# A graph-transformer layer on one core: inputs normalised twice and turned directly, VectorE's first-stage work in another order, four staging rows for keys, mixer weights asked for sooner

## What is computed

```python
xn = _layernorm(x)
x = x + gnn(xn, edges) + mix(xn)          # the two branches read the same xn
x = x + ffn(_layernorm(x))
# gnn(x):
x_norm = _layernorm(x, ln_g, ln_b)        # a second normalisation, on xn
q, k, v = (x_norm @ W + b).reshape(N, 8, 64) for each of Wq, Wk, Wv
ws = (q[src] . k[dst]) * SCALE * edge_attr_8
att = softmax of ws over the edges of one src
values = segment_sum(att * v[dst], src)
return x + (values @ W1 + b1) @ W2 + b2
# mix(x): linear attention with Wq, Wk, Wv, Wp of its own, over all rows
```

## Time and profile before

| | us |
|---|---|
| median of 3 runs (880.22 to 887.66) | 885.28 |
| the profiled execution | 888.54 |
| its span in the trace | 886.8 |
| PE busy | 805.7 (91%) |
| DVE busy | 583.9 (66%) |
| POOL busy | 460.3 (52%) |
| ACT busy | 343.4 (39%) |

### The profile page before, as it was taken

How to read it: one execution, slowest core, us unless ns; L and a number is a source line. 1 busy time by engine, 2 the same in 40 slices (tenths; PEclk the granted TensorE clock), 3 DMA queues, 4 the chain that set the end, 5 groups by cost and what they waited for, 6 DMA issues and landing times.

```text
span 886.8 us, 13753 instructions
## 1 busy us (share of the span) xinstructions
PE 805.7 (91%) x4791; PEld 464.8 (52%) x4791; DVE 583.9 (66%) x1331; ACT 343.4 (39%) x794; POOL 460.3 (52%) x391
## 2 busy tenths in 40 slices
PE   2999997868999999799999999999999999999974
PEld 2554446434456444355555555555556666666642
DVE  3587493924232502277877787888998888788775
ACT  0412301022312131055545555455556555454462
POOL 1038887887878878778778787876100000000000
PEclk9989999988999999889999999999999999999987
DMA  7698999996445476033533535335442323323103
GB/s 220 191 372 273 314 312 306 289 346 205 112 112 159 124 235 215 5 99 99 194 100 111 182 100 193 99 109 181 157 154 100 113 101 105 140 83 105 63 1 116
DMA packets 69635, 144.02 MB, mean 162 GB/s; under 512 B 20537, under 2 KB 54251, under 8 KB 65599
## 3 DMA queue, kind: packets, MB, share of 16 engines
q1 hardware_dynamic: 47084, 119.42, 38.0%
q0 software_dynamic: 13344, 6.28, 6.3%
q10 hardware_dynamic: 9136, 17.39, 5.9%
HBM read 77.99 MB, written 64.77 MB: 161 GB/s over the span
## 4 chain that ended last, share of the span: by engine, by line
PE 66%; DVE 16%; issue 8%; ACT 5%; DMA 4%; ACTq 1%; DVEq 0%
PE bank L890 15%; PE bank L884 10%; DVE AR L1538 9%; PE bank L1099 8%; PE bank L1117 7%; PE bank L1085 7%; PE bank L1145 4%; PE bank L1090 4%; ACT AR L765 3%; DMA AR<-in_L_mix_Wk_dram 2%; PE bank L998 2%; PE bank L873 1%; DMA AR<-in_L_gnn_b_dram 1%; PE bank L987 1%; PE bank L949 1%
## 5 line engine op out<-in xcount | busy, mean ns | idle before, releaser
L514 POOL DMA_INDIRECT w_tab<-pay,idx x330 | 406.3, 1231 | 153.0 <-issue 152.4
L765 ACT ACTIVATE AR<-AR,nmx 128x512 f32<-128x512 f32 (+1 forms) x240 | 159.5, 665 | 179.8 <-DVE nmx L1542 144.4
L1538 DVE CUSTOM_DVE_ANT_0 AR<-bank,AR,MX 128x512 f32<-128x512 f32 (+1 forms) x160 | 151.4, 985 | 23.5 <-PE bank L1090 21.3
L1099 PE MATMUL bank<-ident,AR 128*128 128x128 f32 (+2 forms) x880 | 133.8, 282 | 13.9 <-ACT AR L765 10.5
L1085 PE MATMUL bank<-KT,QT 64*128 64x512 f32 (+1 forms) x480 | 118.8, 572 | 14.3 <-issue 8.6
L1099 PEld LDWEIGHTS bank<-ident,AR 128*128 128x128 f32 (+2 forms) x880 | 98.2, 140 | 61.6 <-ACT AR L765 47.2
L884 PE MATMUL bank<-AR 128*128 128x512 f32 (+1 forms) x288 | 108.6, 537 | 7.8 <-ACT QT L642 3.5
L1117 PE MATMUL bank<-AR,V 128*64 128x128 f32 (+1 forms) x1600 | 114.4, 281 | 0.4 <-DVE AR L1549 0.4
L890 PE MATMUL bank<-AR 128*128 128x512 f32 x240 | 110.4, 616 | 2.5 <-ACT AR L696 2.5
L1538 DVE CUSTOM_DVE_ANT_0 AR<-bank,AR 128x512 f32<-128x512 f32 x80 | 83.9, 1088 | 38.5 <-PE bank L1090 25.8
L587 POOL DMA_INDIRECT AR<-kv_rows,xd x10 | 10.7, 1070 | 188.2 <-PE bank L1117 179.2
(11 more groups left out here) (250 smaller groups left out, 759.2 us busy)
## 6 DMA issues: line engine op xcount, KB each, us to landing
w_tab<-ztile SPq DMA_DIRECT2D x20, 2280.0 KB
AR<-w_tab SPq DMA_DIRECT2D x20, 2048.0 KB
AR<-w_tab SPq DMA_DIRECT2D x10, 1344.0 KB
w_tab<-ztile SPq DMA_DIRECT2D x3, 1800.0 KB
w_tab<-pay,idx POOLq DMA_INDIRECT x330
w_tab<-ztile SPq DMA_DIRECT2D x2, 1700.0 KB
kv_rows<-AR ACTq DMA_DIRECT2D x9, 256.0 KB
kv_rows<-V ACTq DMA_DIRECT2D x9, 256.0 KB
```

Of the source, the lines that this page charges most:

```text
L514: pool.indirect_dma_start(out=w_tab, out_offset=bass.IndirectOffsetOnAxis(ap=idx[:, k, j:j + 1], axis=0), in_=pay[:, k % RING, j, :], in_o ...
L765: act.activation(ws[u % 2][hh][:, 0:n], ws[u % 2][hh][:, 0:n], ACT.Exp, bias=nmx[:, u % 4, hh:hh + 1], accum_out=DG[g][:, c, 2 * p + hh:2 ...
L1099: last = nc.tensor.transpose(bank[2 + hh][0:rws, i * P:(i + 1) * P], ws[u % 2][hh][:, a:a + rws], ident[:, :])
L1538: v.tensor_tensor_reduce(out=ws[u % 2][hh][:, 0:n], in0=bank[SB[(2 * u + hh) % 3]][:, 0:n], in1=Wt[w % 2][:, 0:n, h], scale=1.0, scalar=MX ...
```

## The change

- `normed_twice(j)` writes the rows normalised with both row scales at once (`r12 = r1 * r2`) to the staging tile; PE turns them, and the column scale and shift are applied as they are taken from PSUM (`take_x2`, on ACT, and for piece 0 half on DVE). `spread`, `gain_row` and `fold` go. The rows normalised once are written and turned later, by a second set of transposes per piece.
- DVE's list of the first stage is written in another order: `detect`, the checks, `take_k`, `take_v` and `moments` stand elsewhere; `take_k` and `take_v` of piece 2 are spread over the loser lists.
- Four staging rows for keys instead of two.
- The loads of the mixer's Wk and Wv are issued ahead of the last `k_rows`, `residual(j)` behind `k_rows`. `loser_bases` and `loser_columns` stand earlier on PE.
- The check's copy of the edge weights, `wchk`, lies in tiles 4 to 9 of `V` instead of 0 to 5. `dwin` lies where it was.

The diff, cut to its core:

```diff
-        stg = [ar(19520 + 512 * i, 512) for i in range(2)]
+        stg = [ar(19520, 512), ar(20032, 512), QMN[:, 1760:2272], QMN[:, 2272:2784]]
...
-        wchk = V[0:QL, 0:6, :].rearrange("p t d -> p (t d)")[:, 0:330 * H].rearrange("p (t h) -> p t h", h=H)
+        wchk = V[0:QL, 4:NT, :].rearrange("p t d -> p (t d)")[:, 0:330 * H].rearrange("p (t h) -> p t h", h=H)
...
+            def take_x2(j, ks):
                 t0, n = PIECES[j]
+                if j == 2:
+                    act.wait_ge(s_pr, PROJ_OF["v", 3] + 1)
+                act.wait_ge(s_cols, 1)
+                for k in ks:
+                    tau = TAU_OF["x2", j, k]
+                    act.wait_ge(s_tt, tau + 1)
+                    act.activation(x2T[j % 2][:, k, 0:n * P], bank[tau % 2][:, 0:n * P], ACT.Identity,
+                                   bias=cols[:, 1, k:k + 1], scale=cols[:, 0, k:k + 1]).then_inc(s_ta[tau % 2], 1)
...
             for j in range(3):
                 take_q(j)
                 if j < 2:
-                    gain_row(j + 1)
-                    take_x(j + 1)
+                    take_x2(j + 1, range(KC))
                 if j == 0:
                     roots(2)
-                if j < 2:
-                    residual(j + 1)
+                elif j == 2:
+                    act.dma_start(sMk, wv(mWk)).then_inc(s_mk_l, 16)
+                    act.wait_ge(s_pr, PROJ_OF["k", 2, KC - 1] + 1)
+                    act.dma_start(sMv, wv(mWv)).then_inc(s_mv_l, 16)
+                take_x(j)
                 t0, n = PIECES[j]
                 for t in range(t0, t0 + n):
                     k_rows(t)
+                residual(j)
...
+            def normed_twice(j):
+                t0, n = PIECES[j]
+                a, b = t0, t0 + n
+                if j:
+                    dve.wait_ge(s_tt, TAU_OF[("x2", 0, KC - 1) if j == 1 else ("x", 0, KC - 1)] + 1)
+                dve.wait_ge(s_sq2, j + 1)
+                ch.link(v.reciprocal(r2[:, a:b], sq[:, 1, a:b]))
+                ch.link(v.tensor_tensor(r12[:, a:b], r1[:, a:b], r2[:, a:b], ALU.mult))
+                for i in range(n):
+                    t = t0 + i
+                    v.tensor_scalar(ta[:, i, :], XRES[:, t, :], MV[:, t, 0:1], r12[:, t:t + 1], ALU.subtract, ALU.mult).then_inc(s_xn2, 1)
...
-            normed(0)
             dve.wait_ge(s_cols, 1)
-            take_x(0)
-            fold(0)
+            v.tensor_scalar(qbias[:, :], cols[:, 2, :], SCALE, None, ALU.mult).then_inc(s_qb, 1)
+            normed_twice(0)
+            take_x2(0, (0, 2))
             moments(1)
-            normed(1)
+            normed_twice(1)
             edges()
-            detect(0)
-            detect(1)
-            fold(1)
-            order_checks()
             for m in range(KC):
                 take_k(0, m)
-                detect(2 + m)
+                detect(m)
             moments(2)
-            take_x(1)
-            fold(2)
-            marker_check()
+            normed(0)
+            dve.wait_ge(s_row, 48)
             for t in range(4):
                 take_v(t)
-                if t == 1:
-                    normed(2)
-                detect(6 + t)
+                detect(4 + t)
+            normed_twice(2)
+            order_checks()
+            detect(8)
+            detect(9)
+            normed(1)
+            marker_check()
```

More of the change, by code:

```diff
@@ L87, in link @@
         self.eng.wait_ge(self.sem, self.n)
[L90 removed]
+TAU = [("x2", 0, k) for k in range(KC)]
 for _j, (_t0, _n) in enumerate(PIECES):
     if _j < 2:
[L93 removed]
+        TAU += [("x2", _j + 1, k) for k in range(KC)]
+    TAU += [("x", _j, k) for k in range(KC)]
     TAU += [("k", _t0 + i) for i in range(_n)]
@@ L576, in _ @@
             pool.wait_ge(s_xd, 1)
-            for i in range(2):
-                pool.wait_ge(s_kvst[i], 16 * NT // 2)
+            for i in range(4):
+                pool.wait_ge(s_kvst[i], 16 * ((NT + 3 - i) // 4))
             pool.wait_ge(s_vst, 16 * NT)
@@ L829, in _, with transpose_x @@
             mm = nc.tensor.matmul
-            def spread(j):
+            def transpose_x(what, j):
                 t0, n = PIECES[j]
-                pe.wait_ge(s_r2, j + 1)
-                if j:
-                    pe.wait_ge(s_r2b, j)
-                for i in range(n):
-                    last = nc.tensor.transpose(bank[6][:, i * P:(i + 1) * P], r2[:, t0 + i:t0 + i + 1].to_broadcast([P, P]), ident[:, :])
-                last.then_inc(s_r2p, 1)
-            def take(tau):
-                if tau >= 2:
-                    pe.wait_ge(s_ta, tau - 1)
-            def transpose_x(j):
-                t0, n = PIECES[j]
-                pe.wait_ge(s_xn, t0 + n)
+                pe.wait_ge(s_xn2 if what == "x2" else s_xn, t0 + n)
                 for k in range(KC):
-                    tau = TAU_OF["x", j, k]
-                    take(tau)
+                    tau = TAU_OF[what, j, k]
+                    if tau >= 2:
+                        turned(pe, tau - 2)
                     for i in range(n):
@@ L881, in qk @@
                 for m in range(KC):
+                    if what == "mq" and j == 0 and m == 2:
+                        loser_columns()
                     b = proj((what, j, m))
@@ L1315, in _ @@
                 detect(10 + t)
-            for m in range(KC):
-                take_k(2, m)
-                detect(18 + m)
-            for t in range(8, NT):
-                take_v(t)
-            place_checks()
             def whole(out_, in_, less, per):
@@ L1329, in _ @@
             flat = lambda a: a.rearrange("p k j -> p (k j)")
+            normed(2)
+            for k in range(18, NCH):
+                detect(k)
+            place_checks()
+            take_k(2, 0)
             for i, c in enumerate((dc, oc)):
+                take_k(2, 1 + i)
                 ch.link(v.tensor_tensor(e1, flat(c[:, :, :]), steps1250[0:QL, :], ALU.add))
@@ L1354, in _ @@
             v.tensor_reduce(tot, oc1, AX.X, ALU.add).then_inc(s_tot, 1)
+            take_v(9)
             dve.wait_ge(s_tot, 1)
@@ L1400, in _ @@
             dve.wait_ge(s_pr, PROJ_OF["v", NT - 1] + 1)
-            for i in range(2):
-                dve.wait_ge(s_kvst[i], 16 * NT // 2)
+            for i in range(4):
+                dve.wait_ge(s_kvst[i], 16 * ((NT + 3 - i) // 4))
             for i in range(2):
```

149 lines of the change are left out of this document (52 added, 97 removed).

## The result

| | before | changed |
|---|---|---|
| median, us | 886.47 (880.22 to 888.11, 4 runs) | 11495.80 (11490.46 to 11499.04, 4 runs) |
| span of the profiled execution, us | 886.8 | 11497.3 |
| time over time of before | | 12.99, 95% interval 12.95 to 13.03 |

The change makes the kernel 13 times slower. The flag is set, and every engine runs the general path. That was the forecast: 9850 us, with 7700 to 12,800 around it. The place and the chain were as predicted; a pass takes 31.05 us and not 26, at the upper edge of the 22 to 31 us that the forecast gave it.

The account below looks back on a forecast made before the run. PE, busy 91%, bounds the kernel; the change sets the flag and brings the general path: 616.7 + 50 + 8580 (330 passes of 26 us) + 85 + 515 + 1.7 = 9850 us, range 7700 to 12,800.

Parts of the forecast that it names:

- what the change does to the flag: DVE's first stage: take_k overwrites the destinations' copy in KT before its comparison, 13 of 22 windows; flag is 125.
- The frame of the sum: Time around the loop: entry at 616.7 us, 50 ahead of it, 85 behind, attention 515, 1.7 around the span.
- three gathers: POOL's one-element operation and three gathers at a pass's start: 7.7 us, lower 5.5, upper 12.9.
- scatter: POOL's state scatter of 264 KB at a pass's end: 4.3 us with its one-element operation, lower 3.0.
- handovers: Ten handovers between engines and the loop's registers in a pass: 1.0 us, an estimate.
- The rule of the Trainium skill: 450 KB gather: 2.0 us plus bytes over 436 GB/s, 3.0 us; a pass 3 us shorter, 8850 us in all.
- Rival 3: Long pass: code fetched again at each jump back adds 5 to 9 us, 31 to 35 a pass, 11500 to 12800; 20%.
- its own case: General path's loop: 330 passes of 26 us, 22 to 31 us a pass, 9850 us in all; 60%.
- The quiet flag: Checks still come out 0 and the general path is not run: 867 us; 3%.
- The wait of 3.5 us for ACT goes with four staging rows: PE ahead of the attention stage: its 3.5 us wait goes, part of about 30 us won without the flag.
- the 6.8 us that the loser columns were to save: PE ahead of the attention stage: waits of 6.8 and 2.5 us go with earlier weights and loser columns.
- The cap: Attention stage, tile 10: POOL's pace lets at most 23 us of the lead be kept without the flag.

Follow-up runs that it names:

- e1: The changed kernel with order_checks() directly behind edges(), ahead of the first take_k; 872.54 us, 0.985 of before.
- e2: The kernel before with one move alone, order_checks() behind the four take_k of piece 0; 11467.47 us.
- e3: e1 with column 1 of viol overwritten by ones behind the second check; 11479.62 us.
- e12: The changed kernel in its own order, with the copy of the destinations where no key of piece 0 is written; 0.971 of before.
- e6: The changed kernel with 112 rows instead of 125 in each of a pass's four DMAs; 9585.55 us.
- e7: e1 with detect(0) directly behind edges() and ACT's load of the mixer's Wq issued later, behind roots(2); 869.45 us, 0.981 of before.
- e4: The changed kernel whose passes leave out the gather of the state rows; 11239.62 us.

## Why the prediction was right, and its wrong steps

**The flag** came out as predicted, by the step "what the change does to the flag": e1, e2, e3 and e12 show that the cells shared by `dwin` and the first keys set it, and nothing else. Which of the two comparisons set it, and that it stands at 125, was worked out and not read from any run: the branch asks only whether the flag is over 0.

**The frame of the sum.** Entry at 621.2 us instead of 616.7: POOL's last scatter came 2.9 us later, and from its end to the first DMA of `general()` went 2.9 where I had 1.3 (the rows that I read this from, 221.33 and 222.74, give 1.4). Ahead of the loop 58 instead of 50: POOL stood 24.6 us until the first store of q rows had landed, behind the 2.6 MB of initial state and 1.6 MB of edge data, DMAs that the sum left out; the other stores took 3.4 each instead of 5. Behind it 74 instead of 85 (6.87 us a tile), attention 495 instead of 515: around the loop 1248 us instead of 1267, nothing beside the loop. That the four errors (5 and 8 too little, 11 and 20 too much) partly cancel is luck.

**The pass**, in us, prediction and the pass shown above:

| term | predicted | measured |
|---|---|---|
| copies | 0.5 | 0.49 |
| POOL, three gathers | 7.7 | 10.59 |
| DVE, product, reduction, product | 1.65 | 1.80 |
| PE, 8 matmuls | 3.3 | 3.76 |
| DVE to the exponent, ACT, v times weight | 4.4 | 4.20 |
| PE, values | 2.1 | 2.33 |
| DVE, state | 1.1 | 1.27 |
| POOL, scatter | 4.3 | 6.20 |
| handovers | 1.0 | in the terms |
| sum | 26 | 30.64 |

The steps that failed are the two DMA terms: "three gathers", by 2.9, and "scatter", by 1.9: together the whole difference of 4.6 us and a little more. I took their durations from the 110-row gather in the earlier trace rows and scaled by bytes. The price goes by the engines that the number of rows can be dealt to: 110 has the divisor 11, 125 only 5. With 112 rows the two phases took 7.5 and 3.9 us (e6) and the pass 25.25, close to the 7.7, 4.3 and 26 of the sum. So the chain, the engines and the handovers were right, and the nearest row was the wrong row. The rule of the Trainium skill that I weighed (2.0 us plus bytes over 436 GB/s, "DMA: Bandwidth & Descriptors", section "Anatomy of one DMA — SWDGE (gpsimd) path") would have moved the forecast further off; for the 237 KB of 112 rows an estimate by it is 2.5 us and 3.0 was measured, for 264 KB of 125 rows 2.6 and 5.5.

**Rival 3** named the right total (31 us a pass) for the wrong reason. Nothing in a pass waits for code: DVE's idle time at the loop's head ends with the state's landing, and the same loop with 112 rows takes 25.25 us. And no code is fetched. The page of the changed kernel has two queues for instructions, with 40 and 30 packets; in the 10,180 us of the loop between 720 and 10900 us the only queue with packets is that of POOL's DMAs:

```profile
q8 instruction: 40, 0.66, 0.0%
q14 instruction: 30, 0.25, 0.0%
```

```profile
DMA packets 356529, 421.83 MB, mean 41 GB/s; under 512 B 251861, under 2 KB 251861, under 8 KB 356529
q0 software_dynamic: 356529, 421.83, 14.7%
```

The measured mean of 31.05 us lies just past the line that the prediction drew between its own case and this rival. That it falls inside the stated range comes from the range's room for gathers that follow one another and longer handovers, not from a known price.

**The quiet flag**, 867 us, has e1 as its test: 872.5. The lead at the attention stage's first matmul is 20 us instead of 30:

```profile
71.58 3.77 PE L844 MATMUL bank<-ident,AR 128*128 128x128 f32 x16 [3.64 <-DVE AR L1226]
140.18 9.76 PE L861 MATMUL bank<-AR 128*128 128x256 f32 x32 [3.69 <-ACT QT L648]
160.76 0.39 PE L880 MATMUL bank<-QMN,tri 125*125 125x10 f32 x2 [2.55 <-DVE QMN L1320]
355.05 1.13 PE L1058 MATMUL bank<-KT,QT 64*128 64x512 f32 x4 [2.46 <-DVE AR L1494]
513.27 2.08 PE L1058 MATMUL bank<-KT,QT 64*128 64x512 f32 x4 [8.84 <-DVE MX L1505]
```

(PE's timeline of `e1_checks_ahead`; against 375.27 in the earlier trace rows.) The step that failed is "The wait of 3.5 us for ACT goes with four staging rows": it is still there, 3.69 us. A new one of 3.64 us for DVE's second set of normalised rows (L1226) has come, and of the 6.8 us that the loser columns were to save 2.55 are left. Together these are 9.9 us, about the 10 that are missing. The cap was right in place: PE waits 8.84 us at tile 10. But POOL did not keep its pace. SP's load of the destination windows took 20.1 us to issue instead of 10.9, beside ACT's loads, which are now asked for sooner; with one of these moved back, in e7, it took 17.3. POOL started at 58.8 us instead of 57.2 and issued what was before its scatter of 494.33 us at 499.95. So 15.5 us are left at the end of the span (886.8 - 871.3), not 21.

`e7_destinations_sooner`, at 0.981, is some 2% faster than the kernel before and 13 times faster than the changed one. Whether it is better than e1 is not settled, as their intervals overlap; e12's 0.971 is not read as a time, for the reason given there.

## What to carry to other kernels

Before moving a step in one engine's list, look up what lives in the cells that it and its new neighbours write: no semaphore guards a copy in a shared tile on the engine's own list, and a check that reads wrong cells fails towards the slow path, silently. A guard that has never fired has no price in the profile; price it before touching its inputs. And for an indexed DMA on the critical path choose a number of rows with a large divisor up to 16, here 112 or 120 instead of 124 or 125: 120 rows landed in 3.3 us where 124 took 7.2. The kernels with fewer rows left edges out; to handle all of them by 120 takes 344 passes, by an estimate 344 x 26.39 = 9,080 us against 330 x 31.05 = 10,250.

## What the runs showed that I had not expected

- The time of an indexed DMA goes by the divisors of its number of rows more than by bytes: 237 KB in 3.0 us (112 rows), 254 KB in 3.3 (120), 264 KB in 5.5 (125), 262 KB in 7.2 (124). POOL's own issue goes with it, 0.97, 1.03, 1.23 and 1.36 us.
- Three gathers of 125 rows at once kept 0.5 to 0.6 of the 16 engines busy in their second half, the single scatter 0.1 to 0.3, and the third gather cost only 0.8 us. Their shares lie beside each other: from 5 us behind the first gather's issue on, the commonest number of packets of 2 KB and more in flight is 10 with three gathers and 5 with the two of e4.
- A landing in the profile is not that of its own DMA where several count one semaphore: 4.4 us was shown for kv rows that needed 7.5.
